# f16 retrieval from a split state, with the split on VectorE and the placing on ScalarE

## The reference

```python
x = x + 0.5 * ffn(layernorm(x))
x = x + attn(layernorm(x))
x = x + 0.5 * ffn(layernorm(x))
```

```python
def step(S, inp):
    q_t, k_t, v_t, beta_t = inp
    retrieval = einsum('bhij,bhj->bhi', S, k_t)
    S = S + einsum('bhi,bhj->bhij', beta_t * (v_t - retrieval), k_t)
    o_t = einsum('bhij,bhj->bhi', S, q_t)
    return (S, o_t)
```

## Time and profile before

| | |
|---|---|
| median of 3 runs | 1817.02 us |
| profiled execution | 1815.88 us |
| its span | 1814.2 us |
| instructions | 29738 |
| TensorE busy | 1730.7 us, 95% |
| VectorE busy | 1243.6 us, 69% |
| GpSimd busy | 1209.4 us, 67% |
| ScalarE busy | 1057.8 us, 58% |
| mean granted TensorE clock | 0.995 |

### The profile page before, as it was taken

How to read it: one execution, slowest core, us unless ns; L and a number is a source line. 1 busy time by engine, 2 the same in 40 slices (tenths; PEclk the granted TensorE clock), 3 DMA queues, 4 the chain that set the end, 5 groups by cost and what they waited for, 6 DMA issues and landing times.

```text
span 1814.2 us, 29738 instructions
## 1 busy us (share of the span) xinstructions
PE 1730.7 (95%) x10030; PEld 1068.7 (59%) x10030; DVE 1243.6 (69%) x2890; ACT 1057.8 (58%) x2115; POOL 1209.4 (67%) x1501
## 2 busy tenths in 40 slices
PE   6989989999999999999999999999999999999999
PEld 5855545555555555555555555588655555555588
DVE  5255776777776877868767687777776768777331
ACT  4656565465656565656556474667656565655454
POOL 4463876767676767777676667677776767675653
PEclk9999999999999999999999999999999999999999
DMA  7100000000000000000000000000000000000000
GB/s 290 43 1 1 1 1 1 1 1 2 0 2 0 24 1 24 1 1 1 1 1 1 1 24 1 1 25 1 1 1 1 1 1 13 1 1 12 1 13 13
DMA packets 5270, 23.16 MB, mean 13 GB/s; under 512 B 640, under 2 KB 1664, under 8 KB 3584
## 3 DMA queue, kind: packets, MB, share of 16 engines
q1 hardware_dynamic: 5120, 21.26, 3.2%
HBM read 17.06 MB, written 4.19 MB: 12 GB/s over the span
## 4 chain that ended last, share of the span: by engine, by line
PE 66%; DVE 9%; issue 8%; POOL 8%; ACT 7%; POOLq 0%; DVEq 0%; ACTq 0%
PE ffn_bank L1073 39%; PE ffn_bank L1056 7%; PE att_bank L1121 5%; PE att_bank L1093 4%; POOL hid_lo L565 3%; PE state_bank L1129 2%; PE att_bank L1108 2%; POOL pairs_lo L602 2%; PE ln_bank L1024 2%; PE att_bank L1109 2%; POOL pairs L594 2%; ACT hid L680 2%; DVE hid L821 1%; ACT L680 1%; PE att_bank L1138 1%
## 5 line engine op out<-in xcount | busy, mean ns | idle before, releaser
L1073 PE MATMUL ffn_bank<-hid_hi,w_sb 128*128 128x512 f16 (+1 forms) x2736 | 904.6, 346 | 7.8 <-ACT gate L667 4.6
L1073 PE MATMUL ffn_bank<-hid_lo,w_sb 128*128 128x512 f16 (+1 forms) x2736 | 904.3, 346 | 0.0
L565 POOL TENSOR_TENSOR hid_lo<-hid,hid_hi 128x512 f16<-128x512 f32 (+1 forms) x456 | 463.3, 1032 | 294.8 <-ACT hid_hi L656 294.5
L594 POOL TENSOR_TENSOR pairs<-KQ 128x32 f32<-128x32 f32 (+15 forms) x496 | 326.5, 669 | 122.8 <-DVE KQ L848 104.5
L1073 PEld LDWEIGHTS ffn_bank<-hid_hi,w_sb 128*128 128x128 fp8e4 x2736 | 275.6, 101 | 206.3 <-issue 11.5
L1073 PEld LDWEIGHTS ffn_bank<-hid_lo,w_sb 128*128 128x128 fp8e4 x2736 | 268.2, 98 | 205.4 <-issue 12.7
L602 POOL TENSOR_TENSOR pairs_lo<-pairs,pairs_hi 128x448 f16<-128x448 f32 (+15 forms) x416 | 313.4, 758 | 75.7 <-ACT pairs_hi L728 75.4
L728 ACT CAST pairs_hi<-pairs 128x448 f16<-128x448 f32 (+15 forms) x416 | 175.2, 440 | 158.6 <-POOL pairs L594 157.3
L656 ACT CAST hid_hi<-hid 128x512 f16<-128x512 f32 (+1 forms) x456 | 235.4, 553 | 30.1 <-DVE hid L821 29.4
L680 ACT ACTIVATE hid<-ffn_bank,par_sb 128x512 f32<-128x512 f32 (+1 forms) x304 | 172.1, 617 | 123.1 <-PE ffn_bank L1073 122.4
L1056 PE MATMUL ffn_bank<-xn_hi,w_sb 128*128 128x512 f16 (+1 forms) x608 | 204.7, 351 | 16.3 <-DVE w_sb L770 6.3
(11 more groups left out here) (88 smaller groups left out, 2103.2 us busy)
## 6 DMA issues: line engine op xcount, KB each, us to landing
NK<-in_w SPq DMA_DIRECT2D x11, 1024.0 KB, 5.9
X<-in_x SPq DMA_DIRECT2D x7, 512.0 KB, 3.6
out<-X SPq DMA_DIRECT2D x7, 512.0 KB, 2.6
wqkvb_sb<-in_wqkvb SPq DMA_DIRECT2D x1, 1024.0 KB, 8.4
X<-in_x SPq DMA_DIRECT2D x2, 256.0 KB, 6.4
out<-X SPq DMA_DIRECT2D x2, 256.0 KB, 2.1
wout_sb<-in_wout SPq DMA_DIRECT2D x1, 256.0 KB, 9.2
par_sb<-in_par SPq DMA_DIRECT2D x1, 24.0 KB, 2.4
```

What stands on the lines that cost most here:

```text
L565: pool.tensor_tensor(hid_lo[layer % 2][:, m, call.cols], hid[:, u % HID_BUFFERS, call.cols], hid_hi[layer % 2][:, m, call.cols], ALU.subtr ...
L594: pool.tensor_tensor(packed(pair(pairs, q, dot), n), later, earlier, ALU.mult).then_inc(pairs_made if dot in SPLIT else pairs_ready, 1)
L1073: mm = nc.tensor.matmul(ffn_ps(call, j), weight(name, kk, 2 * pair + i), v[:, kk, cols], start=kk == 0 and part == 0, stop=kk == KT_FF - 1 ...
```

## The change

The state and the keys and queries are split into f16 high and low halves. `KQ_parts` holds the halves of K and Q for a part: ScalarE writes the high one (`high_kq`), GpSimd the low one (`low_kq`, K and Q apart). The state's halves are made in a compact form, `own_parts` (2 x 8 x 32 columns, f16), by VectorE from PSUM (`split_state`: one masked product for the high half, two operations for the low one), and ScalarE places them into the block diagonal `state_parts`, one copy for each 32 partitions (`spread_state`, one tick later). `retrieve` issues, for each of 8 groups, two f16 products, the state's high and low half, each with the high and low halves of keys and queries side by side (64 columns); so a group has two sums, of the operand's high and low half, in 64 PSUM columns instead of 32. VectorE adds the two for the keys with a reduction over the last axis and then does the subtraction and the product in `u_view`; ScalarE copies the queries' two sums apart, to O and `O_low`, and GpSimd adds them at the part's end (`add_o_low`), ahead of VectorE's `add_o`. `save_q` waits for the reduction alone. Ticks: chunk 3 retrieves at 67 instead of 70 and updates at 80 instead of 84; LayerNorm of the attention starts two ticks earlier; the FFN's `apply` and `low` one tick later; four entries of `FRAME_AT` move by 1 or 3. The warm-up matmul reads the f16 zeros.

The diff, without context that says nothing, the new semaphores and the zeroing:

```diff
--- before.py
+++ after.py
@@ -110,7 +110,7 @@
 FRAMES = range(-1, PARTS + 1)
-FRAME_AT = [0, 96, 238, 377, 527, 662, 814, 965, 1117, 1270, 1422, 1574, 1727, 1879, 2031, 2187, 2336, 2488, 2640]
+FRAME_AT = [0, 96, 238, 377, 530, 665, 817, 968, 1117, 1270, 1422, 1574, 1727, 1879, 2031, 2186, 2336, 2488, 2640]
 FIRST_TICK = 0
@@ -136,8 +136,8 @@
 Q_, K_, V_, B_ = range(4)
-E_RETR = [0, 22, 44, 70]
-E_STATE = [15, 35, 58, 84]
+E_RETR = [0, 22, 44, 67]
+E_STATE = [15, 35, 58, 80]
 E_PROJ = {K_: 40, Q_: 51, V_: 47, B_: 43}
@@ -149,6 +149,11 @@
 ACT_LAG, POOL_LAG, DVE_LAG = 2, 3, 1
...
+SPLIT_LAG, SPREAD_LAG = 1, 2
+E_KQ_HIGH, E_K_LOW, E_Q_LOW = 57, 74, 79
+E_O_LOW = 76
@@ -227,7 +232,7 @@
-LN_ATT = dict(sum=18, mean=22, center=24, square=25, sq_sum=27, var=30, root=32, recip=35, norm=37, y_recip=38, apply=38, low=39)
+LN_ATT = dict(sum=16, mean=20, center=22, square=23, sq_sum=25, var=28, root=30, recip=33, norm=37, y_recip=38, apply=38, low=39)
 LN_SECOND = dict(sum=26, mean=30, square=32, sq_sum=36, var=40, root=43, apply=62, low=66)
@@ -319,7 +324,10 @@
         terms = sb("terms", [P, 2, 2 * GB * C])
-        state_bd = sb("state_bd", [P, GB, P])
+        KQ_parts = sb("KQ_parts", [P, 2, 2, COLS], F16)
+        own_parts = sb("own_parts", [P, 2, GB, 32], F16)
+        state_parts = sb("state_parts", [P, 2, GB, P], F16)
+        O_low = sb("O_low", [P, N])
@@ -400,7 +409,7 @@
-            return bank_of("retr", w, c)[:, 0:GB * 2 * C].rearrange("p (g w) -> p g w", w=2 * C)
+            return bank_of("retr", w, c)[:, :].rearrange("p (g a w) -> p g w a", a=2, w=2 * C)
@@ -601,7 +610,23 @@
+            def low_kq(w, which):
+                h = slice(w % HALVES * N, (w % HALVES + 1) * N)
+                pool.wait_ge(kq_hi_ready, w + 1)
+                pool.tensor_tensor(KQ_parts[:, 1, which, h], KQ[:, which, h], KQ_parts[:, 0, which, h], ALU.subtract).then_inc(kq_ready, 1)
+            def add_o_low(w):
+                mine = slice(w % HALVES * N, (w % HALVES + 1) * N)
+                pool.wait_ge(att_read_s, READ["retr", w, HCH - 1])
+                pool.tensor_tensor(O[:, mine], O[:, mine], O_low[:, :], ALU.add).then_inc(o_low_added, 1)
             def attention(f, e):
+                if f + 1 < PARTS and e == E_K_LOW:
+                    low_kq(f + 1, 0)
+                if f + 1 < PARTS and e == E_Q_LOW:
+                    low_kq(f + 1, 1)
+                if 0 <= f < PARTS and e == E_O_LOW:
+                    add_o_low(f)
                 for dot in DOTS_BY[2].get(f * TICKS + e, ()):
@@ -715,9 +740,26 @@
             def save_q(w, c):
-                act.wait_ge(resid_taken, w * HCH + c + 1)
-                act.copy(at_chunk(O[:, :], w, c), retr(w, c)[:, :, C:2 * C]).then_inc(att_read_s, 1)
+                if c == 0 and w:
+                    act.wait_ge(o_low_added, w)
+                act.wait_ge(resid_ready, (w * HCH + c) * 2 + 1)
+                queries = retr(w, c)[:, :, C:2 * C, :]
+                act.copy(at_chunk(O[:, :], w, c), queries[:, :, :, 0])
+                act.copy(O_low[:, c * GB * C:(c + 1) * GB * C].rearrange("p (g t) -> p g t", t=C), queries[:, :, :, 1]).then_inc(att_read_s, 1)
+            def spread_state(w, c):
+                i = w * HCH + c
+                act.wait_ge(state_lo_ready, 2 * i + 2)
+                for q in range(QUADS):
+                    rows = slice(q * 32, (q + 1) * 32)
+                    act.copy(state_parts[rows, :, :, rows], own_parts[rows, :, :, :]).then_inc(state_ready, 1)
+            def high_kq(w):
+                h = slice(w % HALVES * N, (w % HALVES + 1) * N)
+                act.wait_ge(k_ready, 2 * w + 2)
+                act.wait_ge(att_read_s, READ["proj", w, Q_])
+                act.copy(KQ_parts[:, 0, :, h], KQ[:, :, h]).then_inc(kq_hi_ready, 1)
@@ -734,6 +776,8 @@
                             save_q(f, c)
+                        if e == E_STATE[c] + SPREAD_LAG:
+                            spread_state(f, c)
                         if e == E_RETR[c] + 6:
@@ -742,6 +786,8 @@
                         key_root(f + 1)
+                    if e == E_KQ_HIGH:
+                        high_kq(f + 1)
@@ -897,13 +943,14 @@
-                resid = retr(w, c)[:, :, 0:C]
                 dve.wait_ge(att_filled, U["retr", w, c] + 1)
-                nc.vector.tensor_tensor(resid, at_chunk(V[:, :], w, c), resid, ALU.subtract).then_inc(resid_ready, 1)
-                dve.wait_ge(resid_ready, i + 1)
                 if i:
                     dve.wait_ge(u_saved, i)
-                nc.vector.tensor_tensor(u_view, resid, at_chunk(beta[:, :], w, c), ALU.mult).then_inc(resid_taken, 1)
+                nc.vector.tensor_reduce(u_view, retr(w, c)[:, :, 0:C, :], AX.X, ALU.add).then_inc(resid_ready, 1)
+                dve.wait_ge(resid_ready, i * 2 + 1)
+                nc.vector.tensor_tensor(u_view, at_chunk(V[:, :], w, c), u_view, ALU.subtract).then_inc(resid_ready, 1)
+                dve.wait_ge(resid_ready, i * 2 + 2)
+                nc.vector.tensor_tensor(u_view, u_view, at_chunk(beta[:, :], w, c), ALU.mult).then_inc(resid_taken, 1)
@@ -926,19 +973,22 @@
-            def spread_state(w, c):
+            def split_state(w, c):
                 i = w * HCH + c
+                state = state_ps.rearrange("p (g b w) -> p g b w", b=2, w=D)
+                own = [own_parts[:, part, :, :].rearrange("p g (b w) -> p g b w", b=2) for part in range(2)]
                 dve.wait_ge(dstate_ready, i + 1)
-                nc.vector.tensor_tensor(state_bd[:, :, :].rearrange("p g (q w) -> p g q w", w=32),
-                                        state_ps.rearrange("p (g w) -> p g w", w=32).unsqueeze(2).to_broadcast([P, GB, QUADS, 32]),
-                                        head_ones[:, :].rearrange("p (q w) -> p q w", w=32).unsqueeze(1).to_broadcast([P, GB, QUADS, 32]),
-                                        ALU.mult).then_inc(state_ready, 1)
+                nc.vector.tensor_tensor(own[0], state, side_ones[:, :].unsqueeze(1).unsqueeze(3).to_broadcast([P, GB, 2, D]), ALU.mult).then_inc(state_hi_ready, 1)
                 nc.vector.tensor_copy(at_chunk(U_sb[:, :], w, c), u_view).then_inc(u_saved, 1)
+                dve.wait_ge(state_hi_ready, i + 1)
+                for b in range(2):
+                    nc.vector.scalar_tensor_tensor(own[1][:, :, b, :], state[:, :, b, :], side_ones[:, b:b + 1], own[0][:, :, b, :],
+                                                   ALU.mult, ALU.subtract).then_inc(state_lo_ready, 1)
...
                 dve.wait_ge(qk_summed, (w + 1) * C)
-                dve.wait_ge(att_read_s, READ["retr", w, HCH - 1])
+                dve.wait_ge(o_low_added, w + 1)
                 nc.vector.tensor_tensor(O[:, mine], O[:, mine], O_in[:, :], ALU.add).then_inc(o_ready, 1)
@@ -973,8 +1023,8 @@
                             turn_u(f, c)
-                        if e == E_STATE[c] + 1:
-                            spread_state(f, c)
+                        if e == E_STATE[c] + SPLIT_LAG:
+                            split_state(f, c)
                 if f >= 1:
@@ -1113,12 +1163,14 @@
                 if c == 0:
-                    pe.wait_ge(k_ready, 2 * w + 2)
-                pe.wait_ge(state_ready, w * HCH + c + 1)
+                    pe.wait_ge(kq_ready, 2 * w + 2)
+                pe.wait_ge(state_ready, (w * HCH + c) * QUADS + 1)
                 ps = att_use("retr", w, c)
                     at = ((w % HALVES * HCH + c) * GB + g) * C
-                    mm = nc.tensor.matmul(ps[:, g * 2 * C:(g + 1) * 2 * C], state_bd[:, g, :], KQ[:, :, at:at + C], start=True, stop=True)
+                    for part in range(2):
+                        mm = nc.tensor.matmul(ps[:, g * 4 * C:(g + 1) * 4 * C], state_parts[:, part, g, :], KQ_parts[:, :, :, at:at + C],
+                                              start=part == 0, stop=part == 1)
                 mm.then_inc(att_filled, 1)
```

More of the change, by code:

```diff
@@ L220, in ffn_ln @@
     return dict(sum=at, mean=at + 4, center=at + 5, square=at + 6, sq_sum=at + 7, var=at + 11, root=at + 11,
-                recip0=at + 12, recip1=at + 13, recip2=at + 14, recip3=at + 15, norm=at + 19, apply=at + 20, low=at + 22)
+                recip0=at + 12, recip1=at + 13, recip2=at + 14, recip3=at + 15, norm=at + 19, apply=at + 21, low=at + 23)
 def half_ln(at):
@@ L348, in build @@
             "k_ready", "k_turned", "row_mixed", "pairs_made", "pairs_hi_ready", "pairs_ready", "kz_ready"))
-        resid_ready, resid_taken, u_ready, u_saved, dstate_ready, state_ready = (sem(n) for n in (
-            "resid_ready", "resid_taken", "u_ready", "u_saved", "dstate_ready", "state_ready"))
+        resid_ready, resid_taken, u_ready, u_saved, dstate_ready, state_hi_ready, state_lo_ready, state_ready = (sem(n) for n in (
+            "resid_ready", "resid_taken", "u_ready", "u_saved", "dstate_ready", "state_hi_ready", "state_lo_ready", "state_ready"))
```

(5 more changed lines are left out.)

## The result

The change makes the kernel slower: 1844.18 us median (1841.44 to 1846.38, 4 runs) against 1816.59 (1815.57 to 1817.09, 4 runs), ratio 1.0153, 95% interval 1.014 to 1.0165. The forecast was 1753. The profiled run is the longest of the four, 1846.38 us, and has the lowest mean clock, 0.976; the others have 0.978 to 0.981.

What follows compares the result with a forecast made beforehand. TensorE, busy 95% of the span, was taken as the bound: 1815.9 us less 83 for the shorter retrieval plus 20 for added waits gives 1753 us. The range ran from 1727 to 1797.

Steps and rivals of the forecast that it cites:

- Retrieval pitch: Start-to-start time of the retrieval's f16 load-and-matmul pairs on TensorE: 0.028 us each, 0.45 us for 16.
- work saved: TensorE's retrieval falls from 1.74 to 0.45 us a chunk, in 64 chunks: 83 us saved.
- Rival (b): A run of 16 retrieval pairs is slower: 1783 us at 0.057 a pair, 1827 at 0.10; chance 0.09.
- The state's chain: From state product to next retrieval: longer, but ready 2.3 us ahead in the shortest gap, so covered.
- rival (d): The retrieval on TensorE waits for ScalarE's late placing copies: 1861 us at a mean wait of 2 us; chance 0.03.
- new waits: TensorE waiting for busier feeding engines: one more `pairs_lo` wait of 1.15 us a part, say 20 us.
- The prediction's own sign of being wrong: TensorE's start-to-start saving is there and its idle time has grown by over 50 us.
- The tick changes: Moved ticks add no instruction to TensorE: costed at nothing beyond the forecast's added waits.
- a freer queue: VectorE gains 14 us of work, but up to 83 us of its 123 us wait for the retrieval goes.
- ScalarE's added work: Placing copies 147 us, second copy in `save_q` 17, `high_kq` 17: +181 us, share 59% to about 75%.
- Rival (c): ScalarE's bursts delay the FFN stream: waits of 37 to 74 us for 20, giving 1770 to 1807; chance 0.17.
- The clock: Waits of TensorE can lower its clock to the 1.2 GHz level: two more stretches, 3 us each.

Runs made afterwards that it cites:

- quick: The kernel before the change, its retrieval multiplying only 2 of its 8 groups on TensorE: 1747.71 us, ratio 0.9617.
- the chain: quick with the new ticks, plus ScalarE's wait for VectorE, four copies a chunk, and the next retrieval waiting for them: 1819.16 us over 10 runs.
- the new ticks: quick with all tick constants of the change and nothing else: 1772.55 us, ratio 0.9764.
- the copies alone: quick with four scratch copies of 32x512 f16 a chunk on ScalarE, for which nobody waits: 1760.09 us, ratio 0.9692.

## Why the prediction was wrong

The terms that the trace priced were right. Retrieval pitch: 0.028 taken, 0.029 measured; work saved: 83 taken, 79 measured, since a chunk took 1.704 us before, not 1.74, and takes 0.466 now. Rival (b) doesn't hold here: runs of 16 and of 64 pairs of 64 columns keep 0.029. The Trainium skill ("TensorE: Matmul & The Clock Gate", section "Back-to-back issue gap") gives its 81 ns for 128 columns; for 64 columns the measured 29 ns decides, and a run of such pairs with 128 columns is in none of these kernels. ScalarE was to be 1240 us busy and is 1231.5, GpSimd 1267 and 1269.6, VectorE 1258 and 1263.5. VectorE's wait before the retrieval's reader was to be about 40 us and is 44.6. The state's chain is covered, as forecast (2.7 us of waits before the retrieval); rival (d) is not it.

The step that failed is **new waits**: one wait of 1.15 us a part, 20 us. Measured are 77 us of idle time and 33 us of clock, 110. The prediction's own sign of being wrong came up: the saving is there, and idle time has grown by over 50. In the steady stretch it is 117 us where 60 to 85 were forecast, and `pairs_lo` is not most of it, 34.8 of 153 us in the span. What the runs show in its place:

- "The tick changes ... I cost them at nothing". On quick they cost 25 us by themselves (1748 to 1773), 13 of them by chunk 3's ticks alone, where all eight pairs of its solution now come ahead of row 9's emptying on VectorE. I had read VectorE's share over the whole span (69%) and a freer queue; at chunk 3 its share was 91% before the change already. In the changed kernel the same constants save 15 us against the old ones, because the longer chain of the state needs the gap; so the 25 us are not a part that could be had back by undoing them.
- ScalarE's added work was put beside its idle time, 75% against a bound of 100. Rival (c) came nearest and was priced at 17 to 54 us above the forecast; the chain costs 45 to 47 on quick with the new ticks. It named the FFN stream, though, and most of the new waits are before the dots (33 us before the change, 84 after), fewer before the first FFN layer (22 and 40). The wait that `spread_state` adds was named with what stands behind it, but given no price. Alone, with the old ticks, it costs 9 and the work 12; both as a chain, on top of the new ticks, 45 to 47.
- The remaining 25 us (1819 to 1844) are the 5 us of TensorE's longer retrieval, GpSimd's 58 us and the small parts on VectorE and ScalarE; the run with little work on GpSimd is 12 below. I did not separate the rest, so its cause is open.

The clock was mentioned, with 3 us for each of two stretches, and left out of the sum; the mean clock fell by 0.019. (In the earlier trace rows the clock had fallen at 1298.6, ahead of the wait near 1301 to which the prediction put it down and behind one of 0.93 us.) Over 922 to 928, from the last part of the 2.95 us wait shown above on, it reads 0.50, the 1.2 GHz level:

```profile
922.00:928.00 6.00, 5.36 (x19) 3.47 (x20) 3.57 (x11) 1.63 (x3) 3.65 (x8) 0.50 0.02 4
```

The work in such a stretch takes about twice as long: the eight state products at 923.17 take 1.94 us, those of the earlier trace rows 1.00. Not counting the very end, the changed kernel has 18 such stretches, and each begins in or just behind a wait of PE of 1.6 to 3.8 us. The loss grows with the waits, but not with their total alone: 8 us before, 6 (quick), 22 (new ticks), 28 (chain), 41 (after) with idle times of 103, 122, 131, 172, 181; the copies alone on quick lose 8 at an idle time of 132, and the changed kernel with the old ticks loses 30 at 203.

And the range: four waits a part, 74 us, was called the high end and then left out of it, which ended at 1797. Even that end would have been short.

## What to carry to other kernels

In this schedule, written out by hand, with one engine 95% busy and the others 60 to 70%, the others' idle time was not a reserve: it is where they wait for each other. Price an added or a moved step by the busy share of its engine in the very ticks where it lands (91% at chunk 3, against 69% over the span), and list what then stands ahead of the instruction that the bound engine waits for. An added wait and the work behind it can cost more together than apart (9 and 12 us alone, 45 to 47 as a chain on top of moved ticks). Before offloading the bound engine, run the saving alone: here it showed 69 us at once, and that nearly all the rest was to be looked for in the other queues.

## What was unexpected of the hardware

VectorE's product of 1024 f32 elements from two SBUF operands takes 1.22 us where GpSimd does nothing beside it. In the changed kernel it mostly falls beside an instruction of GpSimd with two inputs: 11 of its 13 instances have one beside them for most of their time and take 1.24 to 2.28 us. The mean of all 13 is 1.707:

```profile
L854 DVE TENSOR_TENSOR xn<-xc,roots 128x1024 f32<-128x1024 f32 x13 | 22.2, 1707 | 0.0
```

Before it was 1.309:

```profile
L808 DVE TENSOR_TENSOR xn<-xc,roots 128x1024 f32<-128x1024 f32 x13 | 17.0, 1309 | 0.0
```

The partner pays too. In the instance at 917.56 (1.92 us) GpSimd's

```profile
918.36 1.59 POOL L611 TENSOR_TENSOR pairs_lo<-pairs,pairs_hi 128x224 f16<-128x224 f32 x1
```

takes 1.59 us, where 0.61 was the mean of that form before. In these rows the one that begins second is lengthened: GpSimd's sum of O, begun at 917.13, took its usual 1.27 us, and in four instances of the kernel before, in which GpSimd's `hid_lo` began 0.5 us after the product, the product kept its 1.22 us and `hid_lo` took 1.71 to 1.78 us in place of 1.18. The Trainium skill ("SBUF — State Buffer", section "Who interferes with whom") says that GpSimd's SBUF ports are VectorE's second pair, under an exclusive lock; the rows agree. How much of the late bank of row 9 this lengthening explains, no run separates. The run with GpSimd's additions on 16 columns bears on it: there the product's mean is 1.289 us, row 9's emptying ends 12.5 us after the retrieval's reader in place of 12.9, and the wait before row 7 is 18.4 us in place of 22.9.

The clock isn't fixed by the program. The ten runs of the chain kernel, with the same instructions, took 1811.87 to 1820.07 us, the shortest at a mean clock of 0.990 and the longest at 0.983.
